# A four-layer graph network on one NeuronCore: softmax sums one step later in layer 2, set-up work moved out of the first stage, biases, 0/1 matrices and norm scales moved between engines in layer 3

## The reference, cut to what matters

```python
x = ln(x + L0(x))   # per edge exp(clip(k[src].q[dst]/sqrt(32))) weights v[src]; sums per target, divided by the sum of weights
x = ln(x + L1(x))   # z = (1+eps)*x + sum of x[src]; r = relu(z@W1+b1)@W2 + b2 + x; relu(ln(r)*gamma + beta)
x = ln(x + L2(x))   # h = x@W; softmax over the edges of a target and its self-loop of leaky(a_src+a_dst);
                    # out = sum(h[src]*alpha) + own alpha*h + bias; + x, ln, *ln_w + ln_b
x = ln(x + L3(x))   # q = x@Wq+bq, k = x@Wk+bk + e, v = x@Wv+bv + e, e = edge_attr@We
                    # softmax over a target's edges; out = sum(v*alpha) + x@Ws + bs
```

## Time and profile before

| | us |
|---|---|
| median of 3 runs | 5031.09 (5024.81 to 5033.5) |
| the profiled execution | 4998.33 |
| its span, first to last instruction | 4996.6 |
| PE busy | 4563.9 (91%) |
| DVE busy | 3986.5 (80%) |
| ACT busy | 2805.1 (56%) |
| POOL busy | 2476.3 (50%) |

### The profile page before, as it was taken

The page is one execution under the profiler, slowest core; times in us unless marked ns, Lnnn a source line. Parts: engine busy times, 40 slices in busy tenths (PEclk is TensorE's granted clock), DMA queues, the critical chain, the costliest instruction groups (busy, mean ns, idle before and its releaser), DMA issues. The chain is left out here.

```text
span 4996.6 us, 90737 instructions
## 1 busy us (share of the span) xinstructions
PE 4563.9 (91%) x21673; PEld 3506.0 (70%) x21722; DVE 3986.5 (80%) x13147; ACT 2805.1 (56%) x6326; POOL 2476.3 (50%) x2462
## 2 busy tenths in 40 slices
PE   4999998779999999999888888888799999699998
PEld 3666664448888888888767777777566666577777
DVE  4777778979999999999859999999855555567666
ACT  1787886545555555555547777777611111366565
POOL 3555551237777777777466666666365554000000
PEclk8999996569999999999979999999899999899999
DMA  6777778954444444444468888787555554677775
GB/s 138 210 225 222 223 223 257 298 187 135 150 152 153 149 148 152 153 153 148 143 184 252 244 244 244 243 243 243 183 172 163 163 164 146 193 228 228 223 228 160
DMA packets 911233, 970.10 MB, mean 194 GB/s; under 512 B 104899, under 2 KB 867258, under 8 KB 910892
## 3 DMA queue, kind: packets, MB, share of 16 engines
q1 hardware_dynamic: 500692, 471.58, 32.9%
q10 hardware_dynamic: 327416, 315.35, 18.6%
q0 software_dynamic: 82784, 179.41, 12.3%
HBM read 654.56 MB, written 363.57 MB: 204 GB/s over the span
## 5 line engine op out<-in xcount | busy, mean ns | idle before, releaser
L1186 POOL DMA_INDIRECT nodes_near_rows<-hh_d,source_row x392 | 394.9, 1007 | 401.3 <-DVE nodes_weighted L1403 292.6
L586 POOL DMA_INDIRECT layer_xg<-in_x,edge_rows x392 | 386.7, 987 | 358.5 <-PE layer_t_ps L627 241.5
L884 POOL DMA_INDIRECT nodes_near_rows<-x_d,nodes_cur x392 | 419.0, 1069 | 238.2 <-POOL nodes_cur L879 170.8
L1542 POOL DMA_INDIRECT edges_xg<-x_d,edge_rows x392 | 372.9, 951 | 264.3 <-PE edges_x_ps L1568 172.6
L485 ACT ACTIVATE nodes_x<-nodes_outer_rows,nodes_outer_shift,nodes_outer_rstd 128x256 f32<-128x256 f32 x784 | 428.0, 597 | 61.1 <-issue 51.4
L1597 ACT ACTIVATE edges_xT<-edges_x_ps 128x512 f32<-128x512 f32 x196 | 117.1, 597 | 524.7 <-PE edges_x_ps L1568 524.7
L1806 PE MATMUL nodes_agg<-w_s,nodes_xT 128*128 128x256 f32 x1568 | 405.5, 381 | 0.0
L1004 PE MATMUL nodes_h_ps<-w_h,nodes_x2T 128*128 128x272 f32 x1568 | 392.2, 393 | 8.1 <-ACT nodes_x2T L1081 8.1
L660 PE MATMUL layer_agg<-layer_msg,layer_hot 128*128 128x264 f32 x784 | 314.2, 540 | 73.5 <-issue 65.7
L642 PE MATMUL layer_kv_ps<-w_kv,layer_xT 128*128 128x512 f32 x784 | 372.3, 597 | 1.0 <-DVE layer_made L751 1.0
L994 PE MATMUL nodes_out_ps<-w_b,nodes_hid 128*128 128x256 f32 x1568 | 371.2, 380 | 1.4 <-DVE nodes_inner_rows L925 0.8
(11 more groups left out here) (223 smaller groups left out, 12341.3 us busy)
## 6 DMA issues: line engine op xcount, KB each, us to landing
nodes_xin<-x_d SPq DMA_DIRECT2D x588, 256.0 KB, 3.8
layer_msg<-msg_d SPq DMA_DIRECT2D x392, 132.0 KB
hh_d<-nodes_hh ACTq DMA_DIRECT2D x196, 264.0 KB, 4.1
nodes_msg<-msg_d SPq DMA_DIRECT2D x392, 132.0 KB, 3.1
x_d<-layer_y ACTq DMA_DIRECT2D x196, 256.0 KB, 3.8
x_d<-nodes_x2b ACTq DMA_DIRECT2D x196, 256.0 KB, 3.5
nodes_hin<-hh_d SPq DMA_DIRECT2D x196, 256.0 KB, 3.9
x_d<-nodes_x ACTq DMA_DIRECT2D x196, 256.0 KB
```

Source lines behind the costliest of these rows:

```text
L586: gp.indirect_dma_start(out=xg[:, c % 8, k, :], out_offset=None, in_=x, in_offset=bass.IndirectOffsetOnAxis(ap=edge_rows[:, c, k:k + 1], a ...
L884: gp.indirect_dma_start(out=near_rows[:, r, h, :], out_offset=None, in_=x1_d, in_offset=bass.IndirectOffsetOnAxis(ap=cur[:, r, h:h + 1], a ...
L1186: gp.indirect_dma_start(out=near_rows[:, u % NR, h, :], out_offset=None, in_=hh_d, in_offset=bass.IndirectOffsetOnAxis(ap=source_row[:, 2 ...
L1542: gp.indirect_dma_start(out=xg[:, c % 8, k, :], out_offset=None, in_=x3_d, in_offset=bass.IndirectOffsetOnAxis(ap=edge_rows[:, c, k:k + 1] ...
```

## The change

- prepare: the targets are cast, transposed and turned into masks without waiting for the sources; the weight products move to layer0 (`weights`, one piece per step from step U0 + 56 on, after loads issued by ACT). Only L2's bias is still split in bf16 parts.
- layer0: the 16 `pairs` DMAs are issued two per step between the loads of units 8 to 15; masks at U0 + 24.
- nodes2: everything from the `shares` part of the softmax on moves one step later, on all engines (own and weighted 15 to 16, the norms' lags 18 ... 22 become 19 ... 23, the store 23 to 24); what comes before (the gathers at lag 0, `tops` at 12, Exp at 12) stays. NR stays 16, HOT is 19.
- edges3: no bias matmul; DVE adds the bias rows in PSUM, and the reduce moves between this add and the add of e.
- nodes3: no bias matmuls; DVE adds the bias row in PSUM; GpSimd makes the 0/1 matrices and, with a power of -1/2, the norm's scale and shift; sums, PE, ACT and loads one step later.

```diff
@@ prepare, vector
-                for k in (1, 0):
-                    ve.wait_ge(edges_in[k], 48)
-                    nc.vector.tensor_copy(ends_f[:, k, :, :], ends_c[:, k, :, :]).then_inc(cast, 1)
+                ve.wait_ge(edges_in[1], 48)
+                nc.vector.tensor_copy(ends_f[:, 1, :, :], ends_c[:, 1, :, :]).then_inc(cast, 1)
...
+                    if mask is below_lo:
+                        ve.wait_ge(edges_in[0], 48)
+                        nc.vector.tensor_copy(ends_f[:, 0, :, :], ends_c[:, 0, :, :]).then_inc(cast, 1)
...
-                link(nc.vector.tensor_tensor(b3[:, 0:D], b3[:, 0:D], rows["L2_gnn_ln_b"][0:3, :], ALU.subtract))
...
@@ layer0, sync
-                sp.wait_ge(lists_out, 16)
-                for h in range(H):
...
                 for u in range(UNITS):
+                    if 8 <= u < 8 + H:
+                        h = u - 8
+                        sp.wait_ge(lists_out, 16)
+                        sp.dma_start(pairs[h * 2 * GU:(h + 1) * 2 * GU, 0:WHOLE, :],
...
@@ layer0, vector
-        MASKS = U0 + 6
+        MASKS, WEIGHTS = U0 + 24, U0 + 56
...
+                    if WEIGHTS <= s < WEIGHTS + 12:
+                        weights(s - WEIGHTS)
@@ nodes2
-        NR, HR, XR, WR, HOT, LATER = 16, 5, 9, 4, 18, 12
+        NR, HR, XR, WR, HOT, LATER = 16, 5, 9, 4, 19, 12
@@ nodes2, gpsimd
-                    u = at(16)
+                    u = at(17)
                     if u is not None:
                         gp.wait_ge(own_done, u + 1)
@@ nodes2, sync
-                    u = at(12)
+                    u = at(13)
...
-                    u = at(14)
+                    u = at(15)
@@ nodes2, tensor
-                    u = at(17)
+                    u = at(18)
...
-                    g = at(14)
+                    g = at(15)
...
-                    u = at(14)
+                    u = at(15)
@@ nodes2, vector
-                    tops, shares = (g // GU if g is not None and g % GU == 0 else None for g in (at(12), at(13)))
+                    tops, shares = (g // GU if g is not None and g % GU == 0 else None for g in (at(12), at(14)))
...
-                    u = at(15)
+                    u = at(16)
@@ edges3, tensor
-                        nc.tensor.matmul(kv_ps[r][:, :], ones3[:, :], bias3[:, 2 * D:4 * D], start=True, stop=False)
@@ edges3, vector
+                        ve.wait_ge(kv_done, num(c) + 1)
+                        nc.vector.tensor_tensor(of_chunk[:, :], of_chunk[:, :], kv_bias[:, :], ALU.add).then_inc(kv_biased, 1)
@@ nodes3, gpsimd 
+                    u = at(16)
+                        for h in range(2):
+                            last = gp.tensor_scalar(hot[:, u % 4, h, :], iota[:, :], target_rel[:, 2 * u + h:2 * u + h + 1], None, ALU.is_equal)
+                    u = at(20)
+                        link(gp.tensor_scalar(ln["spread"][:, b, :], ln["moments"][:, b, :, 1], LN_EPS, None, ALU.add))
+                        link(gp.tensor_tensor(ln["rstd"][:, b, :], ln["spread"][:, b, :], minus_half[:, :], ALU.pow))
+                        link(gp.tensor_tensor(ln["back"][:, b, :], ln["moments"][:, b, :, 0], ln["rstd"][:, b, :], ALU.mult))
+                        gp.tensor_scalar(ln["shift"][:, b, :], ln["back"][:, b, :], -1.0, None, ALU.mult).then_inc(ln["shifted"], 1)
@@ nodes3, vector
+                        nc.vector.tensor_tensor(in_halves(agg[u % 4]), in_halves(agg[u % 4]), both(rows["L3_gnn_bs"]), ALU.add).then_inc(based, 1)
@@ nodes3, tensor
-                            nc.tensor.matmul(to, ones3[:, :], bias3[:, D:2 * D], start=False, stop=False)
```

More of the change, by code:

```diff
@@ L218, in marked, with row @@
         return mark, settle
+    def row(ap, n, parts=P):
+        return bass.AP(ap.tensor, ap.offset, [[0, parts], [1, n]])
     def prepare(sb, ps, sem, sems, block):
@@ L666, in _ @@
             def _(act):
+                for k, name in enumerate(("L2_gnn_att_src", "L2_gnn_att_dst")):
+                    act.dma_start(att[:, k, :], row(a[name], D)).then_inc(more_in, 16)
+                for k, name in enumerate(split_biases):
+                    act.dma_start(b3[:, k * D:(k + 1) * D], row(a[name], D, 3)).then_inc(more_in, 16)
                 def body(s, at):
@@ L1547, in _ @@
             def _(sp):
+                for k, name in enumerate(("L3_gnn_bk", "L3_gnn_bv")):
+                    sp.dma_start(kv_bias[:, k * D:(k + 1) * D], row(a[name], D)).then_inc(bias_in, 16)
                 def body(at):
@@ L1581, in body @@
                             pe.wait_ge(joined, num(c) - 3)
[L1582 removed]
                         for j in range(KC):
[L1584 removed]
+                            last = nc.tensor.matmul(kv_ps[r][:, :], xT[:, b, 0, j, :], w3_kv[:, j, :], start=j == 0, stop=j == KC - 1)
                         last.then_inc(kv_done, 1)
@@ L1666, in nodes3 @@
         x_in, msg_in, stored = sems("x_in", XR), [sems(f"msg_in{k}", 2) for k in range(MR)], sems("stored", 4)
+        based, small = sem("based"), sem("small")
         hot_ready, weighed, x_turned, x_copied, summed, spare_ve = (sem("hot_ready"), sem("weighed"), sem("x_turned"), sem("x_copied"),
@@ L1724, in body @@
                         mark(top_run(g, n, run[0:n, :], score_ps[0:n, 0:P]))
-                    g = group(12)
+                    g = group(13)
                     if g is not None:
@@ L1729, in body @@
                         mark(sum_run(g, n, run[0:n, :], grown[0:n, :]))
-                    g = group(13)
+                    g = group(14)
                     if g is not None:
@@ L1734, in body @@
                         mark(nc.vector.reciprocal(total[0:n, :], total[0:n, :]))
-                    g = group(14)
+                    g = group(15)
                     if g is not None:
@@ L1778, in body @@
                         nc.tensor.transpose(score_ps[0:n, 0:P], score[:, 0:n], ident[:, :]).then_inc(score_turned, 1)
-                    g = group(15)
+                    g = group(16)
                     if g is not None:
```

201 lines of the change are left out of this document (107 added, 94 removed).

## The result

The changed kernel takes 5334.67 us (median of 4 runs, 5327.08 to 5335.87), the kernel before, beside it on the same chip, 5030.78 us (4 runs). The ratio is 1.0603, with a 95% interval of 1.0584 to 1.0621: slower by 304 us. The prediction was 5275 us, slower, with a range up to 5340: the measured time lies 60 us above the forecast and just inside the range.

A forecast was written before the change was run, and what follows sets the result against it. PE bounds edges3 and nodes3, a chain of waits nodes2. 4998.3 + 355 - 43 - 39 - 28 = 5243 us profiled, plus 33 carried over: about 5275 us, range 5065 to 5340.

The forecast's parts named there:

- nodes2, +355: nodes2: the loop of waits closes after 2 steps instead of 3 and TensorE's clock falls; 14.5 us per group, +355 us.
- The loop's six terms: nodes2: weighted to gather, gathers and own + x, PE's stretch, DVE's stretch and two hand-overs, together 11.72 us.
- The hand-over from the own matmul to DVE's own: nodes2: passing from PE's own matmul to DVE in the loop, estimated at 0.1 us.
- The clock's fall: nodes2: PE drops to 1.2 GHz after waits of 2.48 us; 2.0 us per two steps, bounds 0 and 2.64.
- The softmax': nodes2: tops, shares and PE's share transposes lengthen the loop's even turns, 3.4 us per group.
- the clock holds: Rival, nodes2: the loop closes in two steps but the waits don't bring the clock down; 5077 us, 20%.
- Faster: Rival, POOL's queue in nodes2: the loop does not decide, later softmax sums save 28 us; 4893 us, 14%.
- edges3, -43: edges3: PE loses one bias matmul per chunk, 0.22 us times 196, with DVE's added work covered; -43 us.
- nodes3, -39: nodes3: PE loses two half-size bias matmuls per unit, -43, GpSimd's work hidden, +4 at start and end; -39 us.
- the 2.5 that I had named as the sign: nodes3: a sign of the forecast, POOL busy under 2.5 us per unit.
- Start, -28: prepare and layer0: -18 us in prepare, -11 in layer0, moved weight products up to +3; sum -28 us.
- Layer0's 11 us: layer0: PE's 7.88 us wait for messages behind 16 DMAs, with slow matmuls after it; -11 us, bounds 0 and -17.

The follow-up runs named there:

- the second trace of before: The kernel before, unchanged, run and traced once more on a slower chip: 5028.06 us.

## Why the prediction came out

**nodes2, +355 against +412.** The mechanism is the one named: two cures that touch nothing but the loop's length in steps (the order on GpSimd, two buffers) remove the loss, and one buffer less makes it without the change. What was off are sizes, and with these rows the group of 62.0 us closes:

- *The loop's six terms* were 11.72. Five hold to within 0.05 us, TensorE's 3.77 us in the steps at full clock. The hand-over from the own matmul to DVE's own, estimated at 0.1 us, is mis-sized: it is 0.89 less the 0.33 us that the tops' max takes, 0.56 us. DVE's own stands behind two short operations of the outer norm, and these wait for ScalarE's root, which waits for e_row, which waits for TensorE's attention matmuls of the same step. That branch runs beside the own matmul and ends a little later. In two of the other pairs it is 0.89 with a piece of the softmax of 0.33 ahead of it, and 0.59; in the fourth, where the share transposes delay the own matmul, it is 0.04. So the mis-size is 0.46 + 0.46 + 0.49 - 0.06 = 1.4 us per group.
- *The clock's fall* was taken as 2.0 us, with 2.64 as its upper bound. From the sum to the end of the own matmul it took 5.52 and 5.53 us behind waits of 2.62 and 3.00, so 1.75 above the 3.77 at full clock; behind the waits of 3.70 and 3.48 it took 6.75 and 7.97 us (0.9 of the latter is the share transposes), so about 3.0 and 3.3. The mean is 2.45. The 87 long waits of the whole stage give a mean of 2.3. The price isn't set by the wait alone: behind waits of 3.0 us it is 1.75 in most cases and 2.9 in five, behind waits of 3.7 us 2.4 to 3.1. A single row of before could not show that. 4 x 0.45 = 1.8 us per group.
- *The softmax'* 3.4 us is what is left: 62.0 - 4 x 11.72 - 4 x 2.45 - 1.4 = 3.9.

Over the stage the group is 59.5 us and not 62.0, and before it was 43.0 and not the 43.74 of the one I took: 16.5 us longer, times 24.4 = 402. Against the second trace of before, 1043.6 us, it is 406. At full clock the forecast was low by 53 to 79 us. The hand-overs are 1.4 x 24.4 = 34 us of it, the softmax 12 and the shorter group of before 18, together 64. The rival "the clock holds" is out at its premise. "Faster" named the right place, GpSimd's queue; its price behind it came out by luck (28 us for the later sums, where 18 were measured).

**edges3, -43.** 43 us between the two traces that can be compared, 34 by the runs of it alone. Between chunks 20 and 180 one takes 3.02 us, where it took 3.24: 0.22 less, as forecast. VectorE's add is hidden, as its 465 busy of 630 us say.

**nodes3, -39 against -55.** The bias matmuls' 43 us are there: a unit without softmax takes 3.03 us, where it took 3.25. From the first to the last start of the matmuls with w_s the stage went from 694.6 us (4294.7 to 4989.3 before) to 640.2 (4685.3 to 5325.5). What I left out is TensorE's wait at the group's turn, which shrank since VectorE has less ahead of its product; its row in the waits of nodes3, after (before it was 45.0 us in 24 waits):

```profile
PE nodes_share_ps L1833 <- DVE nodes_weighted L1764: 35.3, 24, 1.5
```

GpSimd was near to being the bound. Groups of its instructions after:

```profile
L1734 POOL TENSOR_SCALAR nodes_hot<-iota,target_rel 128x128 f32<-128x128 f32 x392 | 234.7, 608 | 44.2 <-PE nodes_agg L1855 44.0
L1743 POOL TENSOR_TENSOR nodes_ln_rstd<-nodes_ln_spread,nodes_minus_half 128x2 f32<-128x2 f32 x196 | 140.9, 719 | 16.3
L1745 POOL TENSOR_SCALAR nodes_ln_shift<-nodes_ln_back 128x2 f32<-128x2 f32 x196 | 46.2, 235 | 18.1
L1742 POOL TENSOR_SCALAR nodes_ln_spread<-nodes_ln_moments 128x2 f32<-128x2 f32 x196 | 43.2, 220 | 87.5 <-DVE nodes_ln_moments L436 79.0
```

The power took 719 ns, twice my 370, but the three other small operations only 201 to 235, and a 0/1 matrix 608 where I had 350. A unit costs GpSimd 2.6 us, not 2.2, and above the 2.5 that I had named as the sign, but still under TensorE's 3.

**Start, -28.** 27 us by the runs on the fastest chip, some 18 on the two slower ones. The prepare part is about 16 us: layer0's first transposes start at 45.1 us instead of 60.7. Layer0's 11 us are mis-sized for most chips. From its first transposes to its last sum it takes 993.3 to 1000.7 us with the new start on the fastest chip, against 1006.4 there with the old one. On the others and in the changed kernel it takes 1006.1 to 1013.0, against 1007.7 to 1011.4: hardly less. TensorE's wait of 7.88 us for messages, from which I took the term, is in the trace of before on record and, longer, in one with the old start on the fastest chip; no trace with the old start on the slower chips has it. The three parts outside nodes2 were to give 110 us and gave 107, but a start that is too large and a nodes3 that is too small cancel there: in that the close agreement is luck.

**The 33 us** between the profiled execution and the median, carried over: the other parts' sum was right against the median. Some 30 of the 33 us are two once-only waits that the execution on record had not or had shorter: VectorE's first wait for the fifths at the head of nodes2, 23.4 us there and 37.2 in the second trace of before, and the one of edges3 above, with 646.6 - 630.5 = 16 us for the stage.

## What to carry to other kernels

Before an operation is moved by a step, write down the loops of waits that it is part of, with the number of steps over which each closes: here a product one step later took a loop of 11.7 us from three steps to two, and 3.9 us per step, which no view of before showed as a cost, became 5.9. The cure is as cheap as the fault: one more buffer or two at the place where the oldest data is given back, or the late operation ahead of the waiting one in an in-order queue. With either, the same change goes from 6.0% slower to 1.7% (the order) or 2.7% (two buffers) faster. Only the second makes the later sums worth having: with nodes2 left as it was the rest of the change is 2.1% faster.

## What was not expected of the hardware

- Half-speed stretches are not of one length: over 87 waits of 2.6 us and more each cost 2.3 us in the mean, and behind waits of the same 3.0 us sometimes 1.75 and sometimes 2.9. Six unused matmuls in each wait made the changed kernel 3.3% faster than with the waits empty.
- The same kernel takes 5001 us on one chip and 5025 to 5030 on others. In the second trace of before, from a slower one, ScalarE stands idle once for 17.6 us near the head of edges3, and TensorE waits 12.4 us behind it; every trace from a slower chip has such a wait of TensorE (10 to 13 us) and none from the fastest has; what holds ScalarE there is open. A part of a change worth 0.3% can't be read from two traces of different chips.
- On GpSimd a 128x2 power costs 719 ns and a 128x2 product of two tiles 201: three and a half times, on the same number of elements.
